# Batch 0's query projection in three f32r terms, with loads, roundings and first scores rearranged around it

## What is computed

```python
query = jnp.einsum('bnc,dc->bnd', teacher_features, Wq) + bq
key = jnp.einsum('bnc,dc->bnd', teacher_features, Wk) + bk
energy = jnp.einsum('bnd,bmd->bnm', query, key)
attention = jax.nn.softmax(energy, axis=-1)
x_m = jnp.einsum('bln,bmn->blm', teacher_logits, attention)
...
x = x + jnp.tanh(g_xattn[0]) * _L0_xattn_ref(_layernorm(x, axis=-1), ctx_1024, ...)
x = x + jnp.tanh(g_ffn[0]) * _L0_ffn_ref(_layernorm(x, axis=-1), ...)
```

## Time and profile before

| | us |
|---|---|
| median of 3 runs | 125.0 |
| lowest, highest | 124.33, 125.34 |
| profiled execution, its own time | 124.74 |
| span of the profiled execution | 122.8 |
| TensorE busy | 116.8 (95%) |
| VectorE busy | 94.7 (77%) |
| GpSimd busy | 93.2 (76%) |
| ScalarE busy | 87.3 (71%) |

### The profile page before, as it was taken

The page is one execution under the profiler, slowest core; times in us unless marked ns, Lnnn a source line. Parts: engine busy times, 40 slices in busy tenths (PEclk is TensorE's granted clock), DMA queues, the critical chain, the costliest instruction groups (busy, mean ns, idle before and its releaser), DMA issues.

```text
span 122.8 us, 1884 instructions
## 1 busy us (share of the span) xinstructions
PE 116.8 (95%) x564; PEld 94.9 (77%) x564; DVE 94.7 (77%) x188; ACT 87.3 (71%) x186; POOL 93.2 (76%) x106
## 2 busy tenths in 40 slices
PE   5989999999999999999999999999999999999960
PEld 4658788888887988878888887888898888888850
DVE  1069599897898995879957984799669939988592
ACT  2365999999999979377998794759987952445100
POOL 3006999918067998999986999985559999999950
PEclk9999999999999999999999999999999999999997
DMA  4998999814814310027761302557000022220035
GB/s 104 222 341 292 400 388 320 313 35 177 237 36 136 97 74 5 3 85 261 270 238 29 142 5 85 171 171 256 0 3 3 5 85 85 85 85 0 0 140 202
DMA packets 10649, 17.15 MB, mean 140 GB/s; under 512 B 1808, under 2 KB 2576, under 8 KB 10640
## 3 DMA queue, kind: packets, MB, share of 16 engines
q1 hardware_dynamic: 9648, 16.91, 40.6%
q10 hardware_dynamic: 992, 0.14, 0.7%
HBM read 12.59 MB, written 4.19 MB: 137 GB/s over the span
## 4 chain that ended last, share of the span: by engine, by line
PE 92%; DVE 4%; issue 1%; ACT 1%; DVEq 0%; ACTq 0%
PE ps_y L387 37%; PE ps_ffn L400 23%; PE ps_score L347 8%; PE ps_turn L354 6%; PE ps_score L354 3%; PE ps_score L461 3%; PE ps_y L354 2%; PE ps_y L317 2%; PE ps_turn L317 2%; PE ps_ffn L317 2%; PE ps_ffn L326 2%; PE ps_turn L347 1%; PE ps_ffn L485 1%; DVE ffn L832 1%; DVE ctx_sb L836 1%
## 5 line engine op out<-in xcount | busy, mean ns | idle before, releaser
L889 POOL TENSOR_TENSOR xt_lo<-xt_raw,xt_hi 128x512 fp32r<-128x512 f32 x16 | 21.1, 1320 | 5.8 <-ACT xt_hi L532 2.9
L387 PE MATMUL ps_y<-pt_hi,xt_hi 128*128 128x512 f32 x64 | 18.1, 404 | 0.0
L387 PE MATMUL ps_y<-pt_hi,xt_lo 128*128 128x512 f32 x64 | 17.5, 395 | 0.0
L387 PE MATMUL ps_y<-pt_lo,xt_hi 128*128 128x512 f32 x64 | 17.5, 395 | 0.0
L400 PE MATMUL ps_ffn<-w_sign,zt_hi 128*128 128x512 f32 x60 | 17.2, 408 | 0.0
L400 PE MATMUL ps_ffn<-w_sign,zt_lo 128*128 128x512 f32 x60 | 16.5, 396 | 0.0
L520 ACT ACTIVATE prob<-ps_score,neg_max 128x512 f32<-128x512 f32 x14 | 9.6, 686 | 9.6 <-DVE neg_max L670 9.6
L742 DVE SCALAR_TENSOR_TENSOR ffn<-ps_ffn,rstd,gain 128x512 f32<-128x512 f32 x15 | 11.2, 745 | 4.9 <-PE ps_ffn L400 3.1
L387 PEld LDWEIGHTS ps_y<-pt_hi,xt_lo 128*128 128x128 f32 x64 | 12.0, 188 | 2.9
L387 PEld LDWEIGHTS ps_y<-pt_lo,xt_hi 128*128 128x128 f32 x64 | 12.0, 188 | 2.9
L894 POOL TENSOR_TENSOR ctx_lo<-ctx_sb,ctx_hi 128x1024 fp32r<-128x1024 f32 x3 | 7.2, 2406 | 8.3 <-DVE ctx_hi L688 8.2
(11 more groups left out here) (177 smaller groups left out, 273.7 us busy)
## 6 DMA issues: line engine op xcount, KB each, us to landing
xt_raw<-in_x_t_dram SPq DMA_DIRECT2D x16, 256.0 KB, 2.9
ctx_sb<-in_ctx_t_dram SPq DMA_DIRECT2D x8, 256.0 KB, 5.5
x_sb<-in_x_dram SPq DMA_DIRECT2D x8, 256.0 KB, 5.3
ctx_sb<-in_x_dram SPq DMA_DIRECT2D x8, 256.0 KB, 6.7
out_dram<-x SPq DMA_DIRECT2D x8, 256.0 KB, 2.0
out_dram<-ctx_sb SPq DMA_DIRECT2D x7, 256.0 KB, 2.0
w_raw<-in_weight_t_dram SPq DMA_DIRECT2D x4, 256.0 KB, 8.2
ln_w<-in_ln_weight_dram SPq DMA_DIRECT2D x1, 256.0 KB, 8.4
```

The source lines that it names most:

```text
L387: mm = pe.matmul(ps_y[t % 2][:, :], lhs[:, t, k, :], rhs[:, k, :], start=(k == 0 and i == 0), stop=(k == KN - 1 and i == 2))
L889: nc.gpsimd.tensor_tensor(xt_lo[:, t, :, :], xt_raw[:, t, :, :], xt_hi[:, t, :, :].bitcast(f32), ALU.subtract).then_inc(xt_lo_done, 1)
```

## The change

Batch 0's queries are projected in three f32r terms, like the other batches'. For that, context 0 is split too: ScalarE makes its ctx_hi in two halves, between the roundings of wq and wk, and VectorE its ctx_lo. Both go to the buffers of context 3 (index B - 2), which are filled later. wq is loaded on ScalarE's queue, ahead of the biases. The gates and ln_bias move from ScalarE's queue to SP's, behind x. The first two score tiles are interleaved by term (`first_scores`): both q_hi*k_hi, then both with k_lo, then both with q_lo, each term with its own wait. Context 1 is rounded by GpSimd instead of VectorE, context 2's rounding on ScalarE stands ahead of the first exponential, and GpSimd's copy of context 3 waits for the second half of batch 0's queries. The warm-up is 15 matmuls of 256 columns instead of 7 of 512.

```diff
-    WARM = 7
+    WARM = 15
...
             load_ctx(0)
-            sp.dma_start(wq_sb[:, :, :], wq_t.rearrange("(k p) d -> p k d", p=P)).then_inc(wq_in, 16)
...
                 load_x(0, t)
+            sp.dma_start(gates[:, 0:1], g_xattn.rearrange("(a n) -> a n", a=1).broadcast_to([P, 1]))\
+              .then_inc(gates_in, 16)
+            sp.dma_start(gates[:, 1:2], g_ffn.rearrange("(a n) -> a n", a=1).broadcast_to([P, 1]))\
+              .then_inc(gates_in, 16)
+            sp.dma_start(lnb_col[:, :], ln_bias_t[:, :]).then_inc(gates_in, 16)
...
             def project_q0():
 
-                pe.wait_ge(wq_in, 16)
+                pe.wait_ge(w_lo_done, 1)
                 for bank, cols, ready in q_first:
-                    for k in range(KC):
-                        mm = pe.matmul(bank[:, cols], wq_sb[:, k, :], ctx_sb[:, 0, k, cols],
-                                       start=(k == 0), stop=(k == KC - 1))
+                    for n, (lhs, rhs) in enumerate(((wq_hi, ctx_hi), (wq_lo, ctx_hi), (wq_hi, ctx_lo))):
+                        for k in range(KC):
+                            pe.wait_ge((ctx0_hi_done, ctx0_lo_done)[n // 2], k + 1)
+                            mm = pe.matmul(bank[:, cols], lhs[:, k, :], rhs[:, B - 2, k, cols],
+                                           start=(n == 0 and k == 0), stop=(n == 2 and k == KC - 1))
                     mm.then_inc(ready, 1)
+
+            def first_scores():
+
+                for n, (lhs, rhs) in enumerate(((q_hi, k_hi), (q_hi, k_lo), (q_lo, k_hi))):
+                    pe.wait_ge((proj_hi, proj_lo, proj_lo)[n], (2, 1, 2)[n])
+                    for t in range(HALF):
+                        mm = pe.matmul(score_bank(0, t)[:, :], lhs[:, 0, t * P:(t + 1) * P], rhs[:, 0, :],
+                                       start=(n == 0), stop=(n == 2))
+                        if n == 2:
+                            mm.then_inc(score_ready, 1)
...
-                pe.matmul(ps_score[0][:, :], q_hi[:, B - 1, :P], q_lo[:, B - 1, :],
+                pe.matmul(ps_score[0][:, :2 * P], q_hi[:, B - 1, :P], q_lo[:, B - 1, :2 * P],
...
-            for t in range(T):
+            first_scores()
+            for t in range(HALF, T):
                 scores(0, t)
...
             act.dma_start(wk_sb[:, :, :], wk_t.rearrange("(k p) d -> p k d", p=P)).then_inc(wk_in, 16)
+            act.dma_start(wq_sb[:, :, :], wq_t.rearrange("(k p) d -> p k d", p=P)).then_inc(wq_in, 16)
...
-            act.dma_start(gates[:, 0:1], g_xattn.rearrange("(a n) -> a n", a=1).broadcast_to([P, 1]))\
...
-            act.dma_start(lnb_col[:, :], ln_bias_t[:, :]).then_inc(gates_in, 16)
...
-            for arrived, w, hi in ((wk_in, wk_sb, wk_hi), (wq_in, wq_sb, wq_hi)):
-                act.wait_ge(arrived, 16)
-                nc.scalar.activation(hi[:, :, :], w[:, :, :], ACT.Copy).then_inc(w_hi_done, 1)
+            act.wait_ge(wq_in, 16)
+            nc.scalar.activation(wq_hi[:, :, :], wq_sb[:, :, :], ACT.Copy).then_inc(w_hi_done, 1)
+            for k in range(KC):
+                act.wait_ge(ctx_in[0][k], 16)
+                nc.scalar.activation(ctx_hi[:, B - 2, k, :], ctx_sb[:, 0, k, :], ACT.Copy).then_inc(ctx0_hi_done, 1)
+                if k == 0:
+                    act.wait_ge(wk_in, 16)
+                    nc.scalar.activation(wk_hi[:, :, :], wk_sb[:, :, :], ACT.Copy).then_inc(w_hi_done, 1)
             act.wait_ge(bias_in, 16 * 2)
             round_k0()
             round_q0()
+            round_ctx(2)
             exps(0, 0)
-            round_ctx(2)
...
-            for j, (w, hi, lo) in enumerate(((wk_sb, wk_hi, wk_lo), (wq_sb, wq_hi, wq_lo))):
...
+            for k in range(KC):
+                dve.wait_ge(ctx0_hi_done, k + 1)
+                nc.vector.tensor_tensor(ctx_lo[:, B - 2, k, :], ctx_sb[:, 0, k, :],
+                                        ctx_hi[:, B - 2, k, :].bitcast(f32), ALU.subtract).then_inc(ctx0_lo_done, 1)
...
-            round_ctx(1)
...
+            for k in range(KC):
+                pool.wait_ge(ctx_in[1][k], 16)
+            nc.gpsimd.tensor_copy(ctx_hi[:, 0, :, :], ctx_sb[:, 1, :, :]).then_inc(ctx_hi_done[0], 1)
             rest_ctx(1)
             rest_ctx(2)
+            pool.wait_ge(q_rest_ready, 1)
```

More of the change, by code:

```diff
@@ L154, in flamingo_block_kernel @@
         proj_lo = sem("proj_lo")
+        ctx0_hi_done = sem("ctx0_hi_done")
+        ctx0_lo_done = sem("ctx0_lo_done")
         q_rest_ready = sem("q_rest_ready")
@@ L499, in _ @@
             act.wait_ge(table_done, 1)
-            act.dma_start(gates[:, 0:1], g_xattn.rearrange("(a n) -> a n", a=1).broadcast_to([P, 1]))\
-               .then_inc(gates_in, 16)
-            act.dma_start(gates[:, 1:2], g_ffn.rearrange("(a n) -> a n", a=1).broadcast_to([P, 1]))\
-               .then_inc(gates_in, 16)
-            act.dma_start(lnb_col[:, :], ln_bias_t[:, :]).then_inc(gates_in, 16)
             def round_qk(b, j):
@@ L683, in rest_qk @@
                          .then_inc(proj_lo, 1)
[L685 to L688, removed]
             def stats_x(b, tiles):
@@ L837, in last @@
                              .then_inc(last_out_done, 1)
-            nc.vector.memset(q_lo[:, B - 1, :].bitcast(f32), 0.0).then_inc(later_zeroed, 1)
-            for j, (w, hi, lo) in enumerate(((wk_sb, wk_hi, wk_lo), (wq_sb, wq_hi, wq_lo))):
-                dve.wait_ge(w_hi_done, j + 1)
-                nc.vector.tensor_tensor(lo[:, :, :], w[:, :, :], hi[:, :, :].bitcast(f32), ALU.subtract)\
-                         .then_inc(w_lo_done, 1)
+            nc.vector.memset(q_lo[:, B - 1, :2 * P].bitcast(f32), 0.0).then_inc(later_zeroed, 1)
+            dve.wait_ge(w_hi_done, 1)
+            nc.vector.tensor_tensor(wq_lo[:, :, :], wq_sb[:, :, :], wq_hi[:, :, :].bitcast(f32), ALU.subtract)\
+                     .then_inc(w_lo_done, 1)
+            for k in range(KC):
+                dve.wait_ge(ctx0_hi_done, k + 1)
+                nc.vector.tensor_tensor(ctx_lo[:, B - 2, k, :], ctx_sb[:, 0, k, :],
+                                        ctx_hi[:, B - 2, k, :].bitcast(f32), ALU.subtract).then_inc(ctx0_lo_done, 1)
+                if k == 0:
+                    dve.wait_ge(w_hi_done, 2)
+                    nc.vector.tensor_tensor(wk_lo[:, :, :], wk_sb[:, :, :], wk_hi[:, :, :].bitcast(f32),
+                                            ALU.subtract).then_inc(w_lo_done, 1)
             dve.wait_ge(bias_in, 16 * 2)
@@ L974, in last @@
                 add_ffn(b, 1)
+            nc.gpsimd.memset(q_hi[:, B - 1, :P].bitcast(f32), 0.0).then_inc(later_zeroed, 1)
             nc.gpsimd.memset(neg_half[:, :], -0.5).then_inc(half_done, 1)
-            nc.gpsimd.memset(q_hi[:, B - 1, :].bitcast(f32), 0.0).then_inc(later_zeroed, 1)
             nc.gpsimd.memset(ident[:, :], 0.0).then_inc(ident_done, 1)
```

## The result

The changed kernel takes 125.47 us, median of 20 runs, against 124.94 for the kernel before, also of 20. The ratio is 1.0060, with a 95% interval of 1.0036 to 1.0084: slower. The forecast was 124.8, slightly faster, in a range of 124.2 to 126.1. So the time lies in the range, but on the wrong side of the kernel before. The profiled execution took 125.47 with a span of 123.7, against 124.74 and 122.8 before.

The account below looks back on a forecast made before the run. TensorE, busy 95% of the span, was taken as the bound, with ScalarE close behind. A gain of 0.16 us from the biases' landing, ceiling 0.3 from the gates, gave 124.8 us on the median; range 124.2 to 126.1.

Parts of the forecast that it names:

- Gates and ln_bias moved to SP: Small loads behind x: land at 14.7 (13.5 to 16.7), before the tanh at 14.93; caps the gain at 0.3 us.
- rival 2: Gates land after 15.0 and ScalarE waits at the tanh: +1.0 us for landing at 16.0, +1.7 at most; chance 0.2.
- The biases: bq, behind wq on ScalarE's queue, lands at 7.5 and holds k_hi; scores start at 8.7, gain 0.16 us.
- rival 1: Small transfers not held behind SP's: bq lands by 7.2, weights' chain sets the start, gain 0.4 to 0.76 us; chance 0.22.
- The weights' chain: Before batch 0's scores: wq lands at 5.05, roundings, subtraction and query matmuls follow, scores could start at 8.45.
- The interleaving: First score matmul waits for q_hi alone, k_lo and q_lo come just in time; removes q_lo's share, 0.40 us.
- The rest: Context 1's rounding on GpSimd and context 2's ahead of the first exp, among others: cost 0.
- The f32r queries: Query projection: 12 f32r matmuls 0.12 us apart, 1.4 us against 1.7, 0.3 less on TensorE, not collected at once.
- The warm-up: 15 x 256 columns for 7 x 512: starts some 0.2 us earlier, end equal within 0.1, no gain taken.
- rival 3: Low clock stays through the 12 score matmuls, because of waits in the query projection: +2.4 us, 127.2; chance 0.04.

Follow-up runs that it names:

- e2: Changed kernel with both biases loaded on SP's queue between context 0 and context 1; 124.93 us, ratio 1.0028 to the kernel before.
- e6: Changed kernel with the old warm-up (7 matmuls of 512 columns, full memsets); ratio 1.0108 to the kernel before, from 6 runs.
- e12: Changed kernel with gates and ln_bias loaded on SP ahead of x, biases still behind wq; 124.52 us, ratio 0.9979 to the kernel before.
- e4: Changed kernel with biases on SP behind context 0 and gates and ln_bias on SP ahead of x; 124.52 us, ratio 0.9993.
- e5: Changed kernel with biases on SP behind context 0, gates and ln_bias on SP ahead of x, and the old warm-up; ratio 1.0003.
- e1: Changed kernel with gates and ln_bias back on ScalarE's queue behind its table load; 125.94 us, ratio 1.0102 to the kernel before.
- e8: Kernel before with only its first two score tiles interleaved by term; ratio 1.0006.
- e11: Kernel before with the change's roundings of contexts 1 and 2 and its interleaving of the first two score tiles; median 124.10, ratio 0.9942.
- e3: Changed kernel with biases on SP behind context 0 and gates and ln_bias back on ScalarE's queue; 124.86 us, ratio 1.0014.
- e10: Kernel before with the change's roundings of contexts 1 and 2, first score tile waiting term by term in the old tile order; ratio 0.9962.
- e7: Kernel before with only the new warm-up (15 matmuls of 256 columns, small memsets); ratio 1.0007.

## Why the prediction was wrong

**The step that failed** is the sum in "Gates and ln_bias moved to SP". It had 14.7 for the landing, from 13.4 for the last x tile plus 1.25 for the three small transfers. The last x tile landed at 13.2 (13.4 forecast). ln_bias landed at 16.1, so the three took 2.9, and not the 1.25 that I had worked out from the lost rate of a stretch. The bounds (13.5 to 16.7) hold it. The point from which it decides, 14.93 plus 0.06, was named, and rival 2 gave +1.0 for a landing at 16.0; attend(0, 0) came 0.94 later. So the mechanism of rival 2 came true, and it got 0.2 because the term was sized with the mean rate of three microseconds instead of the time from bk's landing to bq's (1.1 each), which gave the upper bound. The other profiles with the three on SP's queue have the last of the three 1.9 (e2) and 2.5 (e6) behind the last x tile, and 1.9 (e12), 2.4 (e4) and 2.5 (e5) behind the last tile of context 3: nowhere as little as 1.25. e12 puts the price of the late tanh at 0.8% of the time, 1.0 us; the profile of the changed kernel has 0.6 (22.90 against 22.3), which the width of the intervals allows.

**The biases** were mis-sized too: bq was put at 7.5 with bounds of 6.8 to 8.0 and landed at 8.13, 8.0 (e1), 8.36 (e12) and 8.78 (e6). The order of landings had been read rightly from the earlier trace rows. The Trainium skill's rule that an engine round-robins between its queues (DMA: Bandwidth & Descriptors, "Queues, rings and completion order"), from which rival 1 had bq by 7.2, is not what these four landings show. What is seen is the count that marks a landing; in what order the bytes moved, no view shows. The consequence, that the biases and not the weights set the start of the scores, was right (9.26 against a computed 9.2 for 8.0). But this lateness is hidden under the tanh's in the changed kernel, and without the tanh's it costs nothing measurable (e12 against e4).

**The weights' chain** held: wq landed at 5.2 (5.05 forecast), the last ctx_lo of context 0 was done at 7.85 (7.55). Where no operand is waited for, the query matmuls start 0.12 apart, as forecast.

**The interleaving** was credited with 0.4 of its own, "as long as no other engine becomes late behind it". Alone it gives nothing (e8), since GpSimd's ctx_lo of context 1 is late at once. The prediction had this engine under "The rest" at a cost of 0, as something that might get worse; that it was the next thing late in the kernel before it did not see. There the moves of contexts 1 and 2 are worth 0.7 us together with the interleaving (e11).

**The f32r queries** don't pay. With the late transfers mended, the changed kernel is at parity (e4, e5), while interleaving and context moves with plain f32 queries reach 0.9942 (e11). The traces show a floor under the first scores; that it is the whole reason is argued and not shown. With context 0 split and the biases on time the scores start at 8.73, 8.77 and 8.79 for K = 6.61, 6.76 and 6.93 (e3, e2, e5). With plain f32 queries and the terms waited for one by one they start 2.02 to 2.08 behind K, early or late (e8, e10, e11). In e12, with K as early as 5.76, TensorE waits for ctx_hi, and its last query matmuls start no earlier than 8.50:

```profile
8.50 0.40 PE L343 MATMUL ps_y<-ctx_lo,wq_hi 128*128 128x256 f32 x2
```

So the chain of roundings, which the prediction ended at 8.45, throws an early K away. A late one gains little: e4 (K = 7.09) and e5 start 1.95 and 1.86 behind K, 0.1 to 0.2 better than e11, and not the 0.3 that TensorE saves. The spans of e4's 12 runs lie within 122.5 to 123.1, those of e11's within 121.6 to 123.0: the slowest are alike, the fastest are not.

**The warm-up** was rightly taken at nothing (e7), and the low clock of rival 3 did not come: the score matmuls are 0.23 apart (1.69 for six, with the tail). Rival 3 also had it that no row of the trace shows the clock fall; one does, behind the last matmul (0.50 from 122.00 on, below), where it costs nothing.

**What remains open:** why ln_bias took 7.6 us in the changed kernel, 8.1 in e6 and 6.1 in e2, all from behind the same loads of x. Part of it is the last x tile, which landed at 13.2, 14.1 and 12.8. The rest is the 2.9, 2.5 and 1.9 of the small ones themselves, and no run parts that from chance.

## What to carry to other kernels

Price a few transfers of a few hundred bytes in a row by how much later the last of them lands than the large load ahead of them (1.9 to 2.9 us for three in six profiles here), not by their bytes or by the rate lost in a stretch (1.25), and put them on the queue where their slump in rate falls into a stretch in which nobody waits; here three of them ahead of or behind four large tiles made 0.8%. When a wait is taken from the busiest engine, look in the trace for the next operand that it needs and ask when it will be ready: two edits that each measure as nothing may be worth 0.6% together. And before a single profiled execution is compared with another, check with an instruction that both kernels share whether the engine's pace was the same.

## What the runs showed of the hardware

The start of full pace differs between executions: K spans 5.74 to 7.14 over 14 profiled ones. That it is most of the scatter of the kernel before is argued from the following. Of 29 runs of the kernel before, beside e5 to e8, each gives its span and mean granted clock:

```
mean clock   runs   spans, us
0.993-0.994  8      122.1 to 122.4
0.995        3      122.4 to 122.6
0.996        6      122.7 to 122.9
0.997        4      122.9 to 123.1
0.998        2      123.3
0.999-1.000  6      123.5 to 123.7
```

The two go together over 1.6 us of span, the whole range of this set, and that range is close to the 1.4 us of K. The set beside e1 to e4 has an exception, a span of 122.4 with a mean of 1.000. In the profiled execution of before the mean is below 1 only because of the end, where TensorE is done; the stretches of before and of e10_e9_wait_by_term read (us, PE busy, granted clock, DMA share, GB/s):

```profile
122.00:122.80 0.80, 0.00 (x0) 0.50 0.01 1
```

```profile
122.00:123.50 1.50, 0.00 (x0) 0.94 0.26 87
```

K was 6.16 in the first and 7.14 in the second: where the clock falls later behind the last matmul, it had also risen later at the start, and the run is longer by what the keys' projection took longer. The low value at the end costs nothing. So in this table a higher mean clock goes with a slower run. As a mark of an early rise the low value can't be trusted, though: e12 and e6 have the earliest K of all (5.76 and 5.74), and means of 1.000 and 0.998.
